# Expert stages in five groups of batches, with a fixed area of rows for each expert

## The reference

```
x = x + attn_a(layernorm(x))
x = x + ffn(layernorm(x))
x = x + attn_b(layernorm(x))
x = x + ffn(layernorm(x))
```

```
red = x @ w_red                                  # 128 -> 16
wg_n = wg / max(norm(wg, axis=1), 1e-4)
gates = softmax(red @ wg_n.T)                    # 8 logits for each token
idx = argmax(gates)                              # the first of equal ones
score = gates[idx]
h = gelu(x @ w1[idx] + b1[idx])                  # 128 -> 512, w1 is 256 KB an expert
y = h @ w2[idx] + b2[idx]                        # 512 -> 128, w2 is 256 KB an expert
out = y * score
```

## Time and profile before

| | us |
|---|---|
| median of 3 executions | 1189.83 |
| the profiled execution, its own time | 1195.18 |
| its span in the profile | 1193.4 |
| attention | 0 to 378 |
| expert stage 0: first part, scatter, tiles | 379 to 421, 421 to 463, 463 to 577 |
| delta rule, with the barriers around it | 577 to 981 |
| expert stage 1: first part, scatter, tiles | 981 to 1019, 1019 to 1061, 1061 to 1178 |
| the last addition and the output | 1178 to 1193 |

### The profile page before, as it was taken

How to read it: one execution, slowest core, us unless ns; L and a number is a source line. 1 busy time by engine, 2 the same in 40 slices (tenths; PEclk the granted TensorE clock), 3 DMA queues, 4 the chain that set the end, 5 groups by cost and what they waited for, 6 DMA issues and landing times. The chain is left out here.

```text
span 1193.4 us, 25871 instructions
## 1 busy us (share of the span) xinstructions
PE 835.8 (70%) x9151; PEld 591.8 (50%) x9151; DVE 725.1 (61%) x1534; ACT 532.4 (45%) x1191; POOL 559.3 (47%) x692
## 2 busy tenths in 40 slices
PE   4688888888884603999188999477857755029992
PEld 2356555555553202777124785265646652017772
DVE  6667767777677600222364799999999996102223
ACT  4577767777774201444055220355555512014441
POOL 3465755765663063444450010377777900633442
PEclk9989979989987755999688999687897887559997
DMA  5234124224301413666328400000020010136665
GB/s 174 70 132 147 65 92 149 74 80 150 133 20 57 159 44 108 181 187 171 98 55 115 61 1 0 1 0 1 0 70 18 18 36 0 42 102 175 183 178 168
DMA packets 134387, 104.93 MB, mean 88 GB/s; under 512 B 27360, under 2 KB 120480, under 8 KB 134240
## 3 DMA queue, kind: packets, MB, share of 16 engines
q1 hardware_dynamic: 127568, 92.55, 27.9%
q0 software_dynamic: 5120, 10.53, 2.7%
q10 hardware_dynamic: 1600, 0.49, 0.2%
HBM read 57.98 MB, written 38.62 MB: 81 GB/s over the span
## 5 line engine op out<-in xcount | busy, mean ns | idle before, releaser
L672 DVE TENSOR_SCALAR a_mag<-a_pS 128x1024 int32<-128x1024 int32 (+1 forms) x192 | 178.2, 947 | 70.0 <-PE a_pS L872 64.1
L454 ACT ACTIVATE a_pw<-a_mag,a_eps_a 128x1024 f32<-128x1024 f32 (+1 forms) x192 | 173.2, 933 | 51.6 <-DVE a_mag L672 49.8
L1165 POOL DMA_INDIRECT ys_dram<-f_yo,f_who x96 | 92.0, 958 | 141.7 <-DVE f_yo L1365 124.9
L336 POOL TENSOR_TENSOR a_pw<-a_pw,a_decay 128x256 f32<-128x256 f32 x128 | 93.4, 730 | 96.7 <-ACT a_pw L454 95.5
L1353 DVE TENSOR_SCALAR f_ysT<-f_bY,f_b2s 128x256 f32<-128x256 f32 x48 | 23.2, 484 | 174.2 <-PE f_bY L1453 137.6
L872 PE MATMUL a_pS<-a_qf,a_kf 64*64 64x192 bf16 (+3 forms) x1536 | 109.5, 267 | 16.3 <-DVE a_mag L672 15.8
L1157 POOL DMA_INDIRECT xs_dram<-f_xa,f_pos x64 | 61.7, 965 | 93.9 <-DVE f_pos L1338 75.0
L1208 ACT ACTIVATE f_hs<-f_bH,f_b1s 128x256 f32<-128x256 f32 x192 | 75.4, 475 | 67.8 <-PE f_bH L1443 37.9
L2267 PE MATMUL d_c<-d_pb_p,ident 128*128 128x256 f32 x256 | 73.0, 455 | 42.1 <-POOL d_pb_p L1750 42.1
L1433 PE MATMUL f_bA<-ident,f_xs 128*128 128x128 f32 x96 | 21.6, 310 | 115.0 <-DMA f_xs<-xs_dram 64.2
L1443 PE MATMUL f_bH<-f_xsT,f_w1s 128*128 128x256 f32 x384 | 96.0, 395 | 0.0
(11 more groups left out here) (349 smaller groups left out, 1835.8 us busy)
## 6 DMA issues: line engine op xcount, KB each, us to landing
parts_scratch<-a_parts SPq DMA_DIRECT2D x32, 384.0 KB, 3.3
f_w1s<-in_L_ffn_w_dram SPq DMA_DIRECT2D x48, 256.0 KB
f_w2s<-in_L_ffn_w_dram SPq DMA_DIRECT2D x48, 256.0 KB
a_kf<-parts_scratch SPq DMA_DIRECT2D x16, 512.0 KB, 5.1
a_qf<-parts_scratch SPq DMA_DIRECT2D x16, 512.0 KB, 6.5
xs_dram<-blank SPq DMA_DIRECT2D x12, 516.0 KB, 6.0
f_xs<-xs_dram SPq DMA_DIRECT2D x48, 129.0 KB
parts_scratch<-a_parts SPq DMA_DIRECT2D x16, 256.0 KB, 2.5
```

Of the source, the lines that this page charges most:

```text
L336: pool.tensor_tensor(own, own, decay[:, k, m, hf:NP:2, :], ALU.mult)\
L454: act.activation(pw[:, n % 4, 0:N], mag[:, n % 3, 0:N], ACT.Square, bias=eps_a[:, 0:1])\
L672: dve.tensor_scalar(mag[:, n % 3, 0:2 * N].bitcast(I32).rearrange("p (l t) -> p l t", l=2), pS[:, 2 * (n % 2):2 * (n % 2) + 2, 0:N].bitcas ...
L1165: pool.indirect_dma_start(ys_dram[f][:, :], bass.IndirectOffsetOnAxis(ap=who[:, q, a:a + 1], axis=0), yo[:, q, a, :], None).then_inc(ys_ou ...
```

## The change

**Rows.** Each expert now has a fixed area of 4352 rows (`AREA`, all 4096 tokens and one tile more) in one `xs_dram` of 36864 rows that both stages use. A token's row is the start of its expert's area plus its rank among the tokens of that expert, so it needs the counts of earlier tokens alone.

**Groups.** The 8 batches are five groups (`GROUPS`: batches 0, 1, 2-3, 4-5, 6-7). For each group DVE does the layer norm, the choice and the row numbers (`moments`, `variance`, `deviation`, `normalize`, `choose`, `place`), PE the turning, the logits and the ranks, and POOL scatters the group's tiles once its row numbers are there. The groups' steps are interleaved on DVE, ACT and PE in an order written out by hand. ACT hands the counts so far from one group to the next (`counted`).

**Logits token by token.** The turned tokens are now the weights of the product and the gate weights move: 4 products of 128 tokens x 8 a batch. The logits come out with the token in the partition, and the turning back is gone. The ranks are now small products in bf16, one for each tile of the group, added up in PSUM (`ranks`).

**Blank rows.** Instead of blanking all of `xs_dram`, SP writes 256 blank rows past the end of each expert's rows, once the last group is counted (`end_i`, 8 value loads and 8 DMAs a stage), and at the start of stage 0 eight DMAs of 129 KB for the tiles that no expert needs.

**Tiles.** A table `t_row` gives each tile's first row. The loads are split: `weights` (value load of the expert, w1, w2, and one DMA `bs` for both biases) and `rows` (value load of the row, and the rows). The weights of the first four tiles are issued before SP waits for the scatter, the rows of these tiles after it. In the loop a tile has two value loads and four DMAs. On DVE `who` takes two short operations.

What is left of the program (attention, delta rule, the tile work of PE and ACT) does not change but for names and counts of semaphores.

```diff
+GROUPS = ((0, 1), (1, 2), (2, 4), (4, 6), (6, B))
+NG = len(GROUPS)
+AREA = B * T + ST
+IDLE = 2 * SPAN
...
         @block.sync
         def _(sp):
...
-                for i in range(2):
-                    for k in range(NR):
-                        sp.dma_start(xs_dram[i][SPAN * k:SPAN * (k + 1), :].rearrange("(p a) c -> p (a c)", p=P),
-                                     blank[:, :, :].rearrange("p a c -> p (a c)")).then_inc(s["zero_done"], 16)
+                for k in range(IDLE // ST):
+                    at = E * AREA + ST * k
+                    sp.dma_start(xs_dram[at:at + ST, :].rearrange("(p a) c -> p (a c)", p=P),
+                                 blank[:, :, :].rearrange("p a c -> p (a c)")).then_inc(s["zero_done"], 16)
...
+            sp.wait_ge(s["end_done"], f + 1)
+            for e in range(E):
+                row = sp.value_load(end_i[0:1, e:e + 1], min_val=e * AREA, max_val=e * AREA + B * T)
+                sp.dma_start(xs_dram[bass.ds(row, ST), :].rearrange("(p a) c -> p (a c)", p=P),
+                             blank[:, :, :].rearrange("p a c -> p (a c)")).then_inc(s["fill_done"], 16)
+            sp.wait_ge(s["texp_done"], f + 1)
...
+            def weights(r, q, late):
+                g = NS * f + SLOTS * r + q
+                e = sp.value_load(texp[0:1, bass.ds(SLOTS * r + q, 1)], min_val=0, max_val=E - 1)
+                if late:
+                    sp.wait_ge(s["h_sb"], g - SLOTS + 1)
+                sp.dma_start(w1s[:, q, :], w1[bass.ds(e, 1), :, :].rearrange("e p f -> p (e f)"))\
+                    .then_inc(ws_in[q], 16)
+                if late:
+                    sp.wait_ge(s["y_sb"], g - SLOTS + 1)
+                sp.dma_start(w2s[:, q, :, :], w2[bass.ds(e, 1), :, :].rearrange("e (k p) d -> p (e k) d", p=P))\
+                    .then_inc(ws_in[q], 16)
+                sp.dma_start(bs[:, q, :], bT[:, bass.ds(e, 1), :].rearrange("p e k -> p (e k)"))\
+                    .then_inc(ws_in[q], 16)
+
+            def rows(r, q, late):
+                g = NS * f + SLOTS * r + q
+                row = sp.value_load(t_row[0:1, bass.ds(SLOTS * r + q, 1)], min_val=0, max_val=E * AREA + IDLE - ST)
+                if late:
+                    sp.wait_ge(s["x_ps"], g - SLOTS + 1)
+                    sp.wait_ge(s["who_done"], g - SLOTS + 1)
+                sp.dma_start(xs[:, q, :, :], xs_dram[bass.ds(row, ST), :].rearrange("(a p) c -> p a c", p=P))\
+                    .then_inc(xs_in[q], 16)
+
+            for q in range(SLOTS):
+                weights(0, q, f > 0)
+            sp.wait_ge(s["scat_done"], 16 * NT * (f + 1))
+            sp.wait_ge(s["fill_done"], 16 * E * (f + 1))
...
+            for q in range(SLOTS):
+                rows(0, q, f > 0)
+            with sp.Fori(0, NR - 1) as r:
                 for q in range(SLOTS):
...
+                    rows(r + 1, q, True)
+                    weights(r + 1, q, True)
...
         @block.gpsimd
...
+            for g in range(NG):
+                pool.wait_ge(s["pos_done"], NG * f + g + 1)
+                for i in range(NT)[tiles(g)]:
+                    pool.indirect_dma_start(xs_dram[:, :], bass.IndirectOffsetOnAxis(ap=pos[:, i:i + 1], axis=0),
                                             xa[:, i, :], None).then_inc(s["scat_done"], 16)
...
         @block.vector
...
+            choose(0)
+            normalize(1)
+            place(0)
+            moments(2)
+            choose(1)
+            moments(3)
+            variance(2)
+            place(1)
+            deviation(2)
+            normalize(2)
+            moments(4)
+            moments(5)
+            variance(3)
+            choose(2)
+            place(2)
...
+            deviation(4)
+            normalize(4)
+            choose(4)
+            place(4)
+            tables()
+            scores()
...
         @block.tensor
...
+            def logits(b):
...
+                for i in range(TT):
+                    at = E * (TT * (b - GROUPS[g][0]) + i)
+                    ins = pe.matmul(bH[:, g % 4, at:at + E], rT[:, b % 2, P * i:P * i + P], w_gate[:, :],
+                                    start=True, stop=True)
...
+            def ranks(g):
...
+                pe.matmul(bank[:, 0:E * (n + 1)].rearrange("p (i e) -> p i e", e=E), one_row[0:1, :], seen,
+                          start=True, stop=False, skip_group_check=True)
+                pe.matmul(bank[:, 0:E * n].rearrange("p (i e) -> p i e", e=E), before[:, :], oh[:, lo:lo + n, :],
+                          start=False, stop=False, skip_group_check=True)
+                for k in range(n):
+                    ins = pe.matmul(bank[:, E * (k + 1):E * (n + 1)].rearrange("p (i e) -> p i e", e=E), ones[:, :],
+                                    oh[:, lo + k:lo + k + 1, :].broadcast_to([P, n - k, E]), start=False,
+                                    stop=(k == n - 1), skip_group_check=True)
```

More of the change, by code:

```diff
@@ new lines, in give_back @@
+            def give_back(r, q):
+                pool.wait_ge(s["o_sb"], NS * f + SLOTS * r + q + 1)
+                pool.sem_inc(s["give"], 1)
+                for a in range(NC2):
+                    pool.indirect_dma_start(ys_dram[f][:, :], bass.IndirectOffsetOnAxis(ap=who[:, q, a:a + 1], axis=0),
+                                            yo[:, q, a, :], None).then_inc(ys_out[q], 16)
+            with pool.Fori(0, NR) as r:
+                for q in range(SLOTS):
+                    give_back(r, q)
@@ L1227, in _, with run, moments @@
+            def run(r, late=True, last=False):
+                for q in range(SLOTS):
+                    if not (last and q == SLOTS - 1):
+                        x_copy(*before_slot(r, q, -1), late or q >= 1)
+                    gelu(r, q, late or q >= 2)
+            x_copy(0, 0, late=f > 0)
+            run(0, late=f > 0)
+            with act.Fori(1, NR - 1) as r:
+                run(r)
+            run(NR - 1, last=True)
         @block.vector
         def _(dve):
-            def gate_weights():
+            def moments(b):
+                n0 = 2 * NT * f + 2 * TT * b
+                four = range(TT * b, TT * b + TT)
+                for i in four:
+                    dve.bn_stats(stats[:, i, :], x[:, i, :]).then_inc(s["stat_done"], 1)
+                for k, i in enumerate(four):
+                    dve.wait_ge(s["stat_done"], n0 + k + 1)
+                    dve.bn_aggr(mv[:, i, :], stats[:, i, :]).then_inc(s["stat_done"], 1)
@@ L1231, in gate_weights, with normalize, gate_norm @@
+            def normalize(g):
+                dve.wait_ge(s["rstd_ready"], NG * f + g + 1)
+                for i in range(NT)[tiles(g)]:
+                    dve.tensor_scalar(xa[:, i, 0:C], x[:, i, :], mv[:, i, 0:1], rstd[:, 0, i:i + 1],
+                                      ALU.subtract, ALU.mult).then_inc(s["xnf_done"], 1)
+            def gate_norm():
                 dve.wait_ge(s["fw_in"], 64)
@@ new lines, in _ @@
+            for q in range(SLOTS):
+                y_bias(0, q, late=f > 0 or q >= 2)
+                y_out(0, q, late=f > 0)
+            with dve.Fori(1, NR) as r:
+                for q in range(SLOTS):
+                    y_bias(r, q)
+                    y_out(r, q)
+            for i in range(NT if f == 1 else 0):
+                if i % TT == 0:
+                    k = i // TT
+                    dve.wait_ge(row_in[k], 16 * (2 * f + 1))
+                dve.scalar_tensor_tensor(x[:, i, :], ya[:, i, :], score[:, i:i + 1], x[:, i, :],
+                                         ALU.mult, ALU.add).then_inc(s["add_done"], 1)
@@ L1488, in _ @@
-            ffn(f)
-def delta_rule(nc, x, ys_out, ys, keep, row_in, row_done, row_odd, counted, Wq, Wk, Wv, Wgamma, Wf, Wg1, Wg2, Wo, norm_w):
+            logits(0)
+            ranks(0)
+            turn(1)
+            logits(1)
+            ranks(1)
+            for g in range(2, NG):
+                for b in range(*GROUPS[g]):
+                    turn(b)
+                for b in range(*GROUPS[g]):
+                    logits(b)
+                ranks(g)
+            pe.wait_ge(s["texp_done"], f + 1)
@@ new lines, in run @@
+            def run(r, first=False, last=False):
+                for q in range(SLOTS):
+                    if not (last and q == SLOTS - 1):
+                        turn_x(*before_slot(r, q, -1))
+                    late = f > 0 or not first
+                    up(r, q, late or q >= 2)
+                    if not first or q >= 2:
+                        turn_y(*before_slot(r, q, 2), late or q >= 3)
+                    if not first or q >= 1:
+                        down(*before_slot(r, q, 1), late or q >= 2)
@@ L1492, in delta_rule @@
+            turn_x(0, 0, late=f > 0)
+            run(0, first=True)
+            with pe.Fori(1, NR - 1) as r:
+                run(r)
+            run(NR - 1, last=True)
+            turn_y(NR - 1, SLOTS - 2)
+            down(NR - 1, SLOTS - 1)
+            turn_y(NR - 1, SLOTS - 1)
```

(3 more changed lines are left out.)

640 lines of the change are left out of this document (300 added, 340 removed).

## The result

The changed kernel took **1156.95 us** in the median of 5 runs (1149.88 to 1157.40), the kernel before 1186.97 (1184.09 to 1192.73): a ratio of 0.973 (0.970 to 0.976), 30 us less. The profiled execution of the changed kernel was its shortest, 1149.88 us, with a span of 1148.0.

What follows compares the result with a forecast made beforehand. It took the chain of waits through both expert stages as the bound: row numbers then scatter, first product, SP-paced tile loop. First parts -17 and loop +7 gave -10 us, 1180 us against the median, range 1160 to 1205.

Steps and rivals of the forecast that it cites:

- SP's chain: After the last row number, SP issues eight blanks and four tiles' weights: 18.9 us, ending 6.5 us after the scatter lands.
- scaling beside the scatter: Row numbers, groups 2 to 4: POOL's scatters slow DVE's scalings, 9 us a stage (bounds 0 and 11).
- first rival: Row numbers: no blocking between scaling and scatter, 9 us less in each stage, 1163 us; chance 0.22.
- the loop's term: Tile loop paced by SP: 0.18 us more a tile over 19 tiles and 2 stages, +7 us.
- waits for PE: Row numbers: DVE waits for PE five times, between 9 and 16 us by clock, taken as 12.
- DVE's own work: Row numbers in stage 1: moments, scaling and 70 short operations on DVE, together 34 us.
- First parts: Each stage's start to its first product: 8.6 us less in stage 1, 8.5 in stage 0, together 17.
- Second rival: SP's tile loop: second value load brings a second stall, +0.6 us a tile, 1196 us or 1203; chance 0.20.
- The signs named beforehand: What the later profile should show: first scatter, gaps, scalings of 0.6 to 0.7 us, SP's 4.5 to 4.6 us a tile.
- Third rival: Row numbers: one scaling for each scatter, 11 us more in a stage, 1202 us; chance 0.10.

## Why the prediction was wrong, point by point

The direction was right, and so was the path of the first part: row numbers, then SP's chain, then the first product. The step that failed is the term "scaling beside the scatter", +9 us a stage for DVE's scalings being held by POOL's scatters; the runs show no such hold (0 us), as the first rival had it. A second step failed too, the loop's term of +7 us: it took SP for what sets the pace, and that is PE. In the terms of the sum, over both stages: 18 us less for the blocking, 8 more for the waits for PE, 2 less for DVE's own work and 10 less for the loop make 22 less than forecast; the measured gain is 30 instead of 10. The first rival's own 1163 lies 6 us from the measured time in part by luck, since it had the waits 8 us too short and the loop 10 too long.

- **DVE's own work, 34 us: right.** DVE is busy for 30.0 us; with the 70 short gaps of 0.04 that the forecast counted this is 33.
- **Waits for PE, 9 to 16, taken as 12: at the upper end.** 49.0 less some 33 is 16. The 16 logits passes of a group took 3.45 us, at the lower clock level; with the clock at 0.61 in the mean the last row number came 3.3 us earlier in stage 1 (4.8 in stage 0).
- **Scaling beside the scatter, +9 us a stage: zero.** The last row number came at 49.0 instead of 55, with 4 us more waits, 9 us less blocking and 1 us less work. The two rows that bounded this term were a cast of two values and scalings beside POOL's arithmetic; neither was a scaling beside the issue of an indirect DMA. Why a scaling is slower beside POOL's additions (0.72 us in the earlier trace rows) and not here stays open. The Trainium skill, "SBUF — State Buffer", section "Who interferes with whom", says that tensor_scalar can enter modes in which it and a GpSimd instruction exclude each other. For the 24 fp32 scalings of a stage beside indirect DMAs the traces do not show it: eight take 2.14 us with and without, and the scatters keep their pace. Whether these scalings enter such a mode no trace here tells.
- **SP's chain of 18.9 us: right,** 19.7. That SP and not the scatter ends the wait: right, by 6.9 and 7.4 us (6.5 forecast); taking the blanks off it gave 3.1 and 3.4 us a stage before the blanks' own landing took over. The landing of the last scatter, taken as 2.3 us from before, was 3.7 in both stages; it lay behind SP's chain and cost nothing.
- **First parts, 17 us less: 28.5.** The 6 us of the last row number in each stage are the difference.
- **Loop, +7 us: -3.** Two faults. The value load costs SP its 0.7 us, and the DMA that went gave back 0.65 and the 0.15 by which w2 was dearer behind a bias; the net is nothing. And what SP has to do counts only above PE's 3.9 us: in the kernel before it lies just below (3.8), as the one bias DMA showed, which gave SP 0.8 us a tile of waiting and the kernel nothing. The one profile hid this, because its stalls put SP above PE. The prediction took one execution's loop for the kernel's, though that execution was 5 us above the median and the page showed PE only a few per cent behind.
- **Second rival, a second stall: did not happen.** The changed kernel and the two experiments with two value loads and five DMAs a tile show no stall; whether a second value load doubles it in an execution that has one is open. Nor does the stall go with the branch of the loop. The Trainium skill, "Runtime: NRT & Kernel Launch", section "Instruction fetch mechanics", was cited for that reading; here the stall stood at nearly every tile while the branch is taken at every fourth, and two more profiles of the same loop have none.
- **The signs named beforehand.** First scatter at about 10 and 14: 11.3 and 14.2. Starving before the last three groups: 6.2, 1.2 and 1.0 us. SP's 4.5 to 4.6 us a tile did not come: 3.92 and 3.94. The first rival's sign, scalings of 0.26 everywhere, is what the profile shows (0.27).
- **Third rival, 1.2 us a scaling: refuted** by the same rows as the scaling term.

## What to carry to other kernels

Before a loop's pace is costed from one profile, ask whether that execution is typical: where two engines are within a few per cent of each other, compute the own work of each from written-out instructions, and let the larger of the two set the forecast. Overlap pays at most until the next chain in line; count that chain with its DMA issues (here eight blanks and twelve loads, 18 us) and put what does not need it on an idle engine. A bound for contention should come from the same pair of instructions, or stay a range with zero as its likeliest value.

## What the runs showed of the hardware that was not expected

- Scalings of 128x128 fp32 values on DVE took 0.27 us each beside GpSimd's indirect DMAs, one each 1.26 us, and the same without them.
- The DMA of w2 took SP 0.53 us to issue directly behind the bias DMA of 128 pieces of 16 bytes, and 0.38 directly behind w1; so leaving one small DMA out saved 0.8 us a tile and not 0.65.
- With PE busy for 13 of 15 us the granted clock was 0.61 in the mean; it was 1.00 in the loop, where PE was busy for 29.9 of 30.
- The same program had a stall of about half a microsecond behind nearly every value load of SP's loop in one profile of three.
- A blank of 129 KB took 6.0 us to land beside four tiles' weights, where those issued ahead of the weights took at most 3.3 in that stage. The last scatter took 2.3 us to land in the kernel before, 3.7 in the changed kernel and 4.35 with the blanks split (stage 1), both beside such traffic.
